# Two-layer transformer block: the weights of layer 0 prepared beside its first sequence, and a few steps of layer 1's rounds at other pairs

## The chip, the cores and the metric

The kernel is one program on one core of a Trainium2 chip. The time is that of one execution on the device, in microseconds; a kernel is timed in several runs, and their median stands for it. The profile is one more execution, recorded by the hardware.

Engines: PE (TensorE) does matrix products and transposes, PEld is its weight load, DVE is VectorE, ACT is ScalarE, POOL is GpSimd, SP issues transfers. PEclk is the clock that was granted to TensorE, as a share of 2.4 GHz; 0.50 is its lower level, 1.2 GHz.

## What is computed

x has 16 sequences of 512 tokens with 128 features. Two layers run one after the other, each with an attention-like part and a feed-forward part, both fed from the layer norm of x:

```
xn = layernorm(x);  x = x + L0_attn(xn) + L0_ffn(xn)
xn = layernorm(x);  x = x + L1_attn(xn) + L1_ffn(xn)

L0_attn: y = layernorm(xn) * ln1_g + ln1_b;  q, k, v = y @ W + b (128 -> 1024);  g = sigmoid(y @ Wg + bg)
         state = decay * state + k * v (a scan over tokens);  x2 = xn + (g * q * state * scale) @ Wo + bo
         out = x2 + gelu(layernorm(x2) @ W1 + b1) @ W2 + b2
L0_ffn:  h = silu(x w1 s1) * (x w2 s2);  gelu(h h1);  gelu(. h2);  . w3
L1_attn: gated linear attention in chunks of 64, 4 heads, RMS norm of o, gate, @ Wo
L1_ffn:  softmax attention with 16 heads of 8 over all 512 tokens, layer norm, router (one of 4 experts), layer norm
```

Products whose precision matters are made in three parts: each operand is split into a rounded part (_hi) and a rest (_lo), and hi x hi, hi x lo and lo x hi are summed.

## The kernel before

**Layer 0** is `layer0_program`. It has four blocks of engine programs, one after the other, with a barrier between them:

1. constants: SP loads the columns, rows, identity and plain weights, VectorE and ScalarE make small constants (L701 to L715);
2. `prepare_weights` (L41): the weights that are to be split come in five chunks into two raw buffers (SP, L61). For each chunk TensorE multiplies the blocks of 128 columns with a bias vector, 36 products in all, each in two passes of hardware (L70, x72 in the trace). Then ScalarE scales the chunk in place (L80), and VectorE casts it to the high part (L96) and subtracts that for the low part (L98);
3. the bias sums (L731 to L734);
4. `layer0_sequences` (L161): rounds r = -1 to 17. In a round each stage works on another sequence. Stage P (statistics, xn, transposes xT and yT, the gates of the ternary feed-forward) is one sequence ahead of stage M (v, k, g, q products, scan, output product). Round -1 has stage P of the first sequence alone. TensorE's first product of round 0 is `v` of the first sequence, reading yT_hi and w_hi (L353). Within round -1 VectorE has the statistics (L535), GpSimd a chain for 1/sqrt (L615 to L627), VectorE xn and yh (L546, L548), TensorE their transposes (L359), ScalarE the copy xT_hi (L463), VectorE xT_lo (L502), and then four gates with two products each, ScalarE L473 and L435, VectorE L562, L566, L502. Stage W, in rounds 0 to 2, splits weights for layer 1 ("prep" steps), with buffers prep_raw and prep.

**Layer 1** runs in rounds, 16 of which are full; a round has 32 pairs of steps, laid out by hand in `attention_order()`, a table of (pair, stage, step). A stage's step belongs to the sequence that is so many rounds behind. Every engine goes through the table in the same order. Pair p always begins with `score` p (L1325, two products, exponentiated by ScalarE into c_prob, L1444) and `max` p (L1307, two products, reduced by VectorE to c_row_max, L1597). Score p+1 needs exp p to be done, since there is one bank pair for it, and max p+1 needs reduce p. Then come `pv` (L1335), and what the table puts at the pair. The names that matter here:

- h2 n: half of a gate product of the feed-forward, six products (L1196 to L1198), at the pairs H2_AT;
- U, A: the chunk states (L1247, evaluated on VectorE L1559 to L1564) and the in-chunk scores (L1257, masked by VectorE into c_a_sb, L1569);
- xT: transposes of the next sequence (L1214);
- mT 0, m_st 0: transposes of the row maxima (L1313) and their store;
- aoT 3: transposes of the softmax attention's output (L1343); behind them VectorE has the reciprocal (L1603) and the division (L1605);
- oT, gwo: transposes of o (L1282), copied by ScalarE to c_o_f, and the output product (L1289), to which `r1` adds (L1591);
- rank, place: counting tokens per expert (L1296, L1662);
- gz: the first step of pair 0 (L1169).

Products other than score, max and pv take their PSUM bank from a ring of two, banks 6 and 7, in turn: a use waits until the use before it in the same bank was read. A round has 31 such uses.

Of the kernel before, what the change touches and what calls it, by code (L numbers as in the profile page):

```python
# [40 lines left out]
def prepare_weights(nc, name, raw_dram, split_hi, split_lo, chunks, bias_products=None, psum_bias=None, by_dim=(), base=0):  # L41

    widest = max(n for _, n, _ in chunks)
    with ExitStack() as ctx:
        raw = [ctx.enter_context(nc.sbuf_tensor(f"{name}_raw{i}", [P, widest * P], F32)) for i in range(2)]
        loaded = [ctx.enter_context(nc.semaphore(f"{name}_loaded{i}")) for i in range(2)]
        multiplied = ctx.enter_context(nc.semaphore(f"{name}_multiplied"))  # L50
        scaled = ctx.enter_context(nc.semaphore(f"{name}_scaled"))
        hi_done = ctx.enter_context(nc.semaphore(f"{name}_hi_done"))
        lo_done = ctx.enter_context(nc.semaphore(f"{name}_lo_done"))
        block = ctx.enter_context(nc.Block())

        @block.sync
        def _(sp):
            for i, (first, n, _) in enumerate(chunks):
                if i >= 2:
                    sp.wait_ge(lo_done, i - 1)  # L60
                sp.dma_start(raw[i % 2][:, 0:n * P], raw_dram[:, first * P:(first + n) * P]).then_inc(loaded[i % 2], 16)  # L61

        @block.tensor
        def _(pe):
            for i, (first, n, _) in enumerate(chunks):
                pe.wait_ge(loaded[i % 2], 16 * (i // 2 + 1))
                for blk, col, vec in bias_products or []:
                    if first <= blk < first + n:
                        w = raw[i % 2][:, (blk - first) * P:(blk - first + 1) * P]
                        nc.tensor.matmul(psum_bias[:, col:col + 1], w, vec, start=True, stop=True)  # L70
                pe.drain().then_inc(multiplied, 1)

        @block.scalar
        def _(act):
            for i, (first, n, scale) in enumerate(chunks):
                w = raw[i % 2][:, 0:n * P]
                act.wait_ge(loaded[i % 2], 16 * (i // 2 + 1))
                act.wait_ge(multiplied, i + 1)
                if scale is not None:
                    nc.scalar.activation(w, w, ACT.Copy, scale=scale).then_inc(scaled, 1)  # L80
                else:
                    act.drain().then_inc(scaled, 1)

        @block.vector
        def _(dve):
            for i, (first, n, _) in enumerate(chunks):
                w = raw[i % 2][:, 0:n * P]
                at = slice((first - base) * P, (first - base + n) * P)
                if first in by_dim:
                    w = w.rearrange("p (g j d) -> p g d j", j=4, d=8)  # L90
                    hi, lo = (s[:, at].rearrange("p (g d j) -> p g d j", d=8, j=4) for s in (split_hi, split_lo))
                else:
                    hi, lo = split_hi[:, at], split_lo[:, at]
                dve.wait_ge(loaded[i % 2], 16 * (i // 2 + 1))
                dve.wait_ge(scaled, i + 1)
                nc.vector.tensor_copy(hi, w).then_inc(hi_done, 1)  # L96
                dve.wait_ge(hi_done, i + 1)
                nc.vector.tensor_tensor(lo, w, hi.bitcast(F32), ALU.subtract).then_inc(lo_done, 1)  # L98
# [2116 lines left out]
```

## Time and profile before

| | us |
|---|---|
| median of 3 runs | 2697.13 |
| lowest and highest | 2694.82, 2701.45 |
| the profiled execution | 2709.48 |
| its span in the trace | 2707.7 |
| its mean granted clock | 0.956 |
| TensorE busy | 2422.3 (89%) |
| VectorE busy | 1933.5 (71%) |
| ScalarE busy | 1338.1 (49%) |

Layer 0's rounds begin at 74 us, full rounds of layer 1 (from one gwo to the next) at 1141.58 us; the last round ends with the output from GpSimd. In a timeline row the first number is the start, the second how long, and the bracket how long the engine had been idle before and what ended that. "x4" are instructions put together.

### The profile page before, as it was taken

What the parts mean: (1) busy time and instruction counts of PE and PEld (TensorE: products, weight loads), DVE (VectorE), ACT (ScalarE), POOL (GpSimd) and SP (SyncE); (2) the same over time, 40 slices, a digit from 0 to 9 for tenths busy, and PEclk for the clock granted to TensorE, in tenths of its full rate; (3) what the DMA queues carried; (4) which work ended last, traced back from release to release, by engine and by line L of the source; (5) the groups of instructions that cost most, each with busy time, mean ns of one, the idle gap of its engine ahead of it and who ended that gap; (6) DMA issues with size and microseconds to landing.
All of it is one profiled execution on the core that took longest, in us unless ns stands there. A gap on an engine that the chain in (4) does not pass through costs nothing. (4 is left out here: it accounts for less than half of the span.)

```text
span 2707.7 us, 45139 instructions
## 1 busy us (share of the span) xinstructions
PE 2422.3 (89%) x14582; PEld 1672.5 (62%) x14582; DVE 1933.5 (71%) x3706; ACT 1338.1 (49%) x1926; POOL 594.3 (22%) x630
## 2 busy tenths in 40 slices
PE   3899999999999946899999999999999999999596
PEld 2788888888888734654555545554555555554395
DVE  3889888888888713667777777777777777772375
ACT  1444444444444312265666656665666666555242
POOL 0021112111221100102222221213221221212287
PEclk9999999999999968999999999999999999999798
DMA  4334432233223133323343334333333233211463
GB/s 153 125 115 127 127 100 76 76 119 104 80 76 111 43 135 98 101 75 96 118 130 93 86 101 136 99 88 104 117 116 103 82 107 106 65 51 32 140 228 104
DMA packets 195550, 280.31 MB, mean 104 GB/s; under 512 B 21672, under 2 KB 151161, under 8 KB 186880
## 3 DMA queue, kind: packets, MB, share of 16 engines
q1 hardware_dynamic: 189952, 266.47, 32.8%
q0 software_dynamic: 5504, 12.63, 1.3%
q8 instruction: 53, 0.87, 0.1%
q14 instruction: 41, 0.34, 0.0%
HBM read 148.65 MB, written 131.91 MB: 104 GB/s over the span
## 5 line engine op out<-in xcount | busy, mean ns | idle before, releaser
L1597 DVE TENSOR_REDUCE c_row_max<-b_psum 128x2 f32<-128x1024 f32 x512 | 624.3, 1219 | 286.2 <-PE b_psum L1307 264.7
L1444 ACT ACTIVATE c_prob<-b_psum 128x1024 f32<-128x1024 f32 x512 | 524.1, 1024 | 388.0 <-PE b_psum L1325 384.4
L1307 PE MATMUL b_psum<-c_bk,c_bq 24*128 24x512 f32 x1024 | 261.8, 507 | 55.1 <-DVE c_row_max L1597 38.5
L1325 PE MATMUL b_psum<-c_cq,c_ck 25*128 25x512 f32 x1024 | 261.3, 505 | 36.4 <-ACT c_prob L1444 31.5
L1335 PE MATMUL b_psum<-c_prob,c_v_aug 128*32 128x512 f32 x2048 | 283.5, 627 | 0.3
L1325 PEld LDWEIGHTS b_psum<-c_cq,c_ck 25*128 25x128 f32 x1024 | 96.3, 185 | 218.1 <-ACT c_prob L1444 109.7
L353 PE MATMUL a_psum<-a_yT_hi,a_w_hi 128*128 128x512 f32 x512 | 206.8, 404 | 8.3 <-issue 5.9
L353 PE MATMUL a_psum<-a_yT_hi,a_w_lo 128*128 128x512 f32 x512 | 203.7, 398 | 0.0
L353 PE MATMUL a_psum<-a_yT_lo,a_w_hi 128*128 128x512 f32 x512 | 203.6, 398 | 0.0
L1307 PEld LDWEIGHTS b_psum<-c_bk,c_bq 24*128 24x128 f32 x1024 | 97.0, 186 | 108.1 <-DVE c_row_max L1597 82.1
L459 ACT ACTIVATE a_g<-a_psum,a_cols 128x512 f32<-128x512 f32 x64 | 44.1, 689 | 238.5 <-PE a_psum L353 238.5
L517 DVE TENSOR_TENSOR_SCAN a_st_sb<-a_decay,a_kv_sb 128x512 f32<-128x512 f32 x128 | 157.2, 1228 | 4.4
L615 POOL TENSOR_TENSOR a_rs<-a_mv,a_eps 128x4 f32<-128x4 f32 x16 | 3.2, 201 | 664.2 <-DVE a_mv L540 664.2
L376 PEld LDWEIGHTS a_psum<-a_w_plain,a_outs 128*128 128x128 f32 x1024 | 134.3, 192 | 11.8
L1196 PE MATMUL b_psum<-c_g_hi,b_f_hi 128*128 128x512 f32 x256 | 119.4, 467 | 17.7 <-DMA b_f_lo<-f_split_scratch 11.6
L376 PE MATMUL a_psum<-a_w_plain,a_outs 128*128 128x128 f32 x1024 | 135.0, 275 | 0.0
L1749 POOL TENSOR_TENSOR c_o_ms<-c_o_ms,b_minus_half 128x16 f32<-128x16 f32 x16 | 46.6, 2910 | 385.0 <-DVE c_o_ms L1581 385.0
L514 DVE SCALAR_TENSOR_TENSOR a_kv_sb<-a_psum,a_bias,a_v_sb 128x512 f32<-128x512 f32 x128 | 95.5, 746 | 44.0 <-PE a_psum L353 23.2
L353 PEld LDWEIGHTS a_psum<-a_yT_hi,a_w_hi 128*128 128x128 f32 x512 | 97.1, 190 | 29.8 <-issue 8.7
L447 ACT ACTIVATE a_v_sb<-a_psum,a_bias 128x512 f32<-128x512 f32 x128 | 88.7, 693 | 47.2 <-PE a_psum L353 46.2
L353 PEld LDWEIGHTS a_psum<-a_yT_lo,a_w_hi 128*128 128x128 f32 x512 | 97.6, 191 | 23.2
L353 PEld LDWEIGHTS a_psum<-a_yT_hi,a_w_lo 128*128 128x128 f32 x512 | 97.6, 191 | 21.2
(298 smaller groups left out, 5419.9 us busy)
## 6 DMA issues: line engine op xcount, KB each, us to landing
sorted_scratch<-a_pad SPq DMA_DIRECT2D x16, 2184.5 KB, 13.9
g_scratch<-a_g_hi SPq DMA_DIRECT2D x16, 1024.0 KB, 4.0
g_scratch<-a_g_lo SPq DMA_DIRECT2D x16, 1024.0 KB, 7.1
c_g_hi<-g_scratch SPq DMA_DIRECT2D x16, 1024.0 KB, 6.1
c_g_lo<-g_scratch SPq DMA_DIRECT2D x16, 1024.0 KB, 8.1
stack_scratch<-c_qk_hi SPq DMA_DIRECT2D x256, 64.0 KB, 1.6
d_wt<-expert_scratch SPq DMA_DIRECT2D x19, 834.0 KB
c_bq<-stack_scratch SPq DMA_DIRECT2D x128, 96.0 KB
```

Of the source, the lines that this page charges most:

```text
L353: mm = nc.tensor.matmul(out, a, c, start=(n == 0), stop=(n == last))
L376: mm = nc.tensor.matmul(tok[:, cut(t)], outs[:, i % OUTS, cut(t)], blk(w_plain, A_WO + i), start=(i == 0 and t == 0), stop=(i == FB0 - 1), ...
L447: nc.scalar.activation(v_sb[:, i % 2, :], bank(f"v{i}"), ACT.Identity, bias=bias[:, 4 * i:4 * i + 1]).then_inc(S["v"], 1)
L514: nc.vector.scalar_tensor_tensor(out=kv_sb[:, :], in0=bank(f"k{i}"), scalar=bias[:, 4 * i + 1:4 * i + 2], in1=v_sb[:, i % 2, :], op0=ALU.a ...
L517: nc.vector.tensor_tensor_scan(st_sb[:, :], decay[:, i:i + 1].to_broadcast([P, SEQ]), kv_sb[:, :], 0.0, ALU.mult, ALU.add).then_inc(S["sca ...
L1196: nc.tensor.matmul(bank(f"h2{c}"), hi, g1_hi[:, k, :], start=(k == 0), stop=False)
L1307: mm = nc.tensor.matmul(psum[:, MAX + x, :], bq[r, j, cut(t)], bk[r, j, :], start=True, stop=True)
L1325: mm = nc.tensor.matmul(psum[:, SCORE + x, :], ck[r, j, cut(kb)], cq[r, j, :], start=True, stop=True)
L1335: mm = nc.tensor.matmul(psum[32 * g:32 * g + 32, PV, :], v_aug[:, kb, HPG * j + g, :], prob[:, (2 * i + g // 2) % 4, g % 2, :], start=(kb ...
L1444: nc.scalar.activation(prob[:, i % 4, :, :], psum[:, SCORE:SCORE + 2, :], ACT.Exp, scale=DH1 ** -0.5).then_inc(S["exp"], 1)
L1597: nc.vector.tensor_reduce(row_max[:, t, at:at + 3:2], psum[:, MAX:MAX + 2, :], AX.X, ALU.max).then_inc(S["row_max"], 1)
L1749: nc.gpsimd.tensor_tensor(o_ms[:, 2, :], o_ms[:, 1, :], minus_half[:, :], ALU.pow).then_inc(S["o_rms"], 1)
```

## The change

In layer 0 the first three blocks are gone. Their work stands in `layer0_sequences`:

- SP issues, at its start, the loads of cols, the first sequence, the identity, then five raw chunks: s (128x1024), q1 and q2 (128x2048 each), h1 (into the space of a_ga), w1 (128x512), then the plain weights and rows;
- in round -1 ScalarE makes each high part by one Copy with scale from the raw weights (HIGH_BEHIND says behind which step), and VectorE each low part by one instruction raw x column - high (LOW_BEHIND);
- the 36 bias products stand between TensorE's steps of round -1 (BIAS_BEHIND), into bank 7;
- VectorE scales the output weights and adds the biases at the start of round 0; TensorE waits there for all five low parts, the biases and the scaling;
- the preparation for layer 1 uses the raw weights' space, and its first load waits until the last low part and bias product are done.

In layer 1's table h2 4 moves from pair 14 to 13. At the even pairs (2, 4, 6, 10, 16, 20) h2 stands first among the table's steps, at the odd ones last. mT 0 moves from pair 17 to 22, m_st 0 from 19 to 24, the second half of oT from 29 to 30. The ring is turned once in a round: O1 and the use behind it, mT 0, have the same bank, and so the uses before it have the other bank than they had, and gwo and the next round's gz share bank 6. The diff, cut:

```diff
+HIGH_BEHIND = {("stats", 0): ("s", "q1", "q2"), ("gate", 0): ("h1",), ("gate", 1): ("w1",)}
+LOW_BEHIND = {("stats", 0): ("s",), ("xn", 0): ("q1",), ("gate", 0): ("q2",), ("gate", 1): ("h1",), ("gate", 2): ("w1",)}
+BIAS_BEHIND = {("stats", 0): range(0, 8), ("xT", 0): range(8, 12), ("gate", 0): range(12, 18), ("gate", 1): range(18, 24),
+               ("gate", 2): range(24, 30), ("gate", 3): range(30, 36)}
...
+        raw = sb("raw", [P, A_H1 * P])
...
-        prep_raw = sb("prep_raw", [P, HID * P])
-        prep = sb("prep", [P, 2, HID * P], F32R)
+        prep_raw = raw[:, 0:HID * P]
+        prep = raw[:, HID * P:3 * HID * P].rearrange("p (h w) -> p h w", h=2).bitcast(F32R)
...
+            sp.dma_start(cols[:, :], d_cols).then_inc(S["cols_in"], 16)
+            sp.dma_start(xin[:, :, :], x_rows[0]).then_inc(S["x_in"], 16)
+            sp.dma_start(ident[:, :], d_ident).then_inc(S["ident_in"], 16)
+            for name in WEIGHTS:
+                sp.dma_start(raw_of[name], weight(d_split, name)).then_inc(S["raw_" + name], 16)
+            sp.dma_start(w_plain[:, :], d_plain[:, 0:A_W3 * P]).then_inc(S["plain_in"], 16)
+            sp.dma_start(rows[:, :, :], d_rows).then_inc(S["rows_in"], 16)
...
+                if not looped and add == 0:
+                    pe.wait_ge(S["w_lo"], len(WEIGHTS))
+                    pe.wait_ge(S["bias"], 3)
+                    pe.wait_ge(S["wo_scaled"], 1)
...
+                def weights_high(kind, i):
+                    for name in HIGH_BEHIND.get((kind, i), ()):
+                        act.wait_ge(S["raw_" + name], 16)
+                        by = WEIGHTS[name][2]
+                        nc.scalar.activation(weight(w_hi, name), raw_of[name], ACT.Copy,
+                                             scale=col(by) if by else 1.0).then_inc(S["w_hi"], 1)
...
+                def weights_low(kind, i):
+                    for name in LOW_BEHIND.get((kind, i), ()):
+                        dve.wait_ge(S["w_hi"], list(WEIGHTS).index(name) + 1)
+                        by = WEIGHTS[name][2]
+                        nc.vector.scalar_tensor_tensor(out=weight(w_lo, name), in0=raw_of[name], scalar=col(by) if by else 1.0,
+                                                       in1=weight(w_hi, name).bitcast(F32), op0=ALU.mult,
+                                                       op1=ALU.subtract).then_inc(S["w_lo"], 1)
...
-H2_AT = (2, 4, 6, 10, 14, 16, 19, 20)
+H2_AT = (2, 4, 6, 10, 13, 16, 19, 20)
...
+    for n, p in enumerate(H2_AT):
+        if p % 2 == 0:
+            put(p, "F", "h2", n)
     put(0, "C2", "xnb_ld")
...
-    put(17, "B", "mT", 0)
+    put(22, "B", "mT", 0)
...
-    put(19, "B", "m_st", 0)
+    put(24, "B", "m_st", 0)
...
-    put(29, "A1", "oT", 1)
+    put(30, "A1", "oT", 1)
...
+        ring_uses = [u for step in order for u in attention_uses(step)]
...
+        bank_of |= {u: RING[(n + 1) % 2] for n, u in enumerate(ring_uses[:ring_uses.index("O1") + 1])}
```

How the rows stand on the engines. In the fences, a row is the line, the operation, its output and inputs, the shape and the waits. Some semaphores of the hardware are used by several blocks, and then the name printed can be that of another block.

VectorE at the start of the program. Before, from the last chunk of weights to the first statistics:

```order
L96 CAST a_w_hi<-a_raw 128x2048 [waits a_scaled,a_loaded0]
L98 TENSOR_TENSOR a_w_lo<-a_raw,a_w_hi 128x2048 [waits a_hi_done]
L47 UNCONDITIONAL_BRANCH
L729 UNCONDITIONAL_BRANCH [waits barrier_Pool_Activation_PE_DVE_SP_release]
L731 TENSOR_TENSOR a_bias<-a_psum,a_cols 128x32
L732 TENSOR_TENSOR a_bias<-a_psum,a_cols 128x4
L734 TENSOR_SCALAR a_half_bias<-a_bias 128x32 [waits a_bias_done]
L725 UNCONDITIONAL_BRANCH
L487 UNCONDITIONAL_BRANCH [waits barrier_Pool_Activation_PE_DVE_SP_release]
L489 MEMSET a_pad 128x257
L491 MEMSET a_pad 128x1 [waits a_pad_set]
L535 BN_STATS a_stats<-a_xin 128x6 [waits a_x_in]
```

VectorE in the changed kernel, from the last yh of the first sequence:

```order
L583 TENSOR_SCALAR a_yh<-a_xin,a_mv,a_rs 128x128
L524 SCALAR_TENSOR_TENSOR a_w_lo<-a_raw,a_cols,a_w_hi 128x2048 [waits a_w_hi]
L518 TENSOR_TENSOR a_xT_lo<-a_psum,a_xT_hi 128x512 [waits a_xT_hi]
L597 SCALAR_TENSOR_TENSOR a_gate_w<-a_gate_t,a_psum 128x512 [waits a_gate_t]
L601 SCALAR_TENSOR_TENSOR a_h<-a_psum,a_s_half,a_gate_w 128x512 [waits a_gate_w,a_P_filled]
L524 SCALAR_TENSOR_TENSOR a_w_lo<-a_raw,a_cols,a_w_hi 128x2048 [waits a_w_hi]
```

The low parts of the weights, which all stood ahead of the statistics, now stand behind them, between the steps of the first sequence.

TensorE in pairs 13 and 14 of a round, from U on. Before:

```order
L1247 MATMUL b_psum<-c_v_sb,c_kgT 32x64 x12
L1321 REGISTER_ALU
L1325 MATMUL b_psum<-c_cq,c_ck 128x512 x2
L1303 REGISTER_ALU
L1307 MATMUL b_psum<-c_bk,c_bq 128x512 x2
L1164 ISA
L1257 MATMUL b_psum<-c_qg,c_kg 128x128 x8
L1164 REGISTER_ALU
L1196 MATMUL b_psum<-c_g_hi,b_f_hi 128x512
```

TensorE in the changed kernel, from U on:

```order
L1235 MATMUL b_psum<-c_v_sb,c_kgT 32x64 x12
L1152 REGISTER_ALU
L1184 MATMUL b_psum<-c_g_hi,b_f_hi 128x512
L1185 MATMUL b_psum<-c_g_hi,b_f_lo 128x512
L1186 MATMUL b_psum<-c_g_lo,b_f_hi 128x512
L1184 MATMUL b_psum<-c_g_hi,b_f_hi 128x512
L1185 MATMUL b_psum<-c_g_hi,b_f_lo 128x512
L1186 MATMUL b_psum<-c_g_lo,b_f_hi 128x512
L1309 REGISTER_ALU
L1313 MATMUL b_psum<-c_cq,c_ck 128x512 x2
```

The six products of h2 4, which stood behind A (L1257), now stand ahead of score 14; max 14, A, score 15 and max 15 follow without them.

TensorE at the end of a round, from the second half of oT or the rank to gwo. Before:

```order
L1282 MATMUL b_psum<-b_ident,c_o_n 128x128 [waits c_attn]
L1282 MATMUL b_psum<-b_ident,c_o_n 128x128 x3
L1321 REGISTER_ALU
L1325 MATMUL b_psum<-c_cq,c_ck 128x512 [waits c_exp]
L1325 MATMUL b_psum<-c_cq,c_ck 128x512
L1303 REGISTER_ALU
L1307 MATMUL b_psum<-c_bk,c_bq 128x512 [waits c_row_max]
L1307 MATMUL b_psum<-c_bk,c_bq 128x512
L1296 MATMUL b_psum<-c_ahead,c_ones_row 128x20 [waits c_o_f,c_ahead]
L1298 MATMUL b_psum<-c_mask,b_causal 128x16
```

```order
L1289 MATMUL b_psum<-b_w_plain,c_o_f 128x128 [waits c_o_f]
L1289 MATMUL b_psum<-b_w_plain,c_o_f 128x128 x7
L1031 REGISTER_ALU
L1031 COMPARE_AND_BRANCH
L1325 MATMUL b_psum<-c_cq,c_ck 128x512 [waits c_m_in0,c_exp,c_c_in0,c_ones_in]
L1325 MATMUL b_psum<-c_cq,c_ck 128x512
L1307 MATMUL b_psum<-c_bk,c_bq 128x512 [waits c_row_max,c_b_in0]
L1307 MATMUL b_psum<-c_bk,c_bq 128x512
L1169 MATMUL b_psum<-c_xT_hi,b_w_hi 128x512 [waits c_r1]
```

TensorE in the changed kernel at the same places:

```order
L1284 MATMUL b_psum<-c_ahead,c_ones_row 128x20 [waits c_attn,c_ahead]
L1286 MATMUL b_psum<-c_mask,b_causal 128x16
L1270 MATMUL b_psum<-b_ident,c_o_n 128x128 [waits c_o_f]
L1270 MATMUL b_psum<-b_ident,c_o_n 128x128 x3
L1309 REGISTER_ALU
```

```order
L1277 MATMUL b_psum<-b_w_plain,c_o_f 128x128 [waits c_place,c_o_f]
L1277 MATMUL b_psum<-b_w_plain,c_o_f 128x128 x7
L1019 REGISTER_ALU
L1019 COMPARE_AND_BRANCH
L1313 MATMUL b_psum<-c_cq,c_ck 128x512 [waits c_m_in0,c_exp,c_c_in0,c_ones_in]
L1313 MATMUL b_psum<-c_cq,c_ck 128x512
L1295 MATMUL b_psum<-c_bk,c_bq 128x512 [waits c_row_max,c_b_in0]
L1295 MATMUL b_psum<-c_bk,c_bq 128x512
L1157 MATMUL b_psum<-c_xT_hi,b_w_hi 128x512 [waits c_o_f]
```

The second half of oT now stands behind the rank; gwo waits for place besides the copy of o, and gz (the last row) for the copy of o instead of for r.

## Rows read from the trace of the kernel before

**Rows 1.** The page: TensorE busy, share, instructions; granted clock in 40 slices.

```profile
PE 2422.3 (89%) x14582; PEld 1672.5 (62%) x14582; DVE 1933.5 (71%) x3706; ACT 1338.1 (49%) x1926; POOL 594.3 (22%) x630
...
PEclk9999999999999968999999999999999999999798
```

**Rows 2.** Windows of the start: stretch, length, busy (instructions), clock, DMA share, GB/s.

```profile
13.20:46.50 33.30, 15.83 (x72) 15.58 (x72) 13.95 (x13) 4.72 (x3) 0.00 (x0) 1.00 0.21 78
46.50:74.20 27.70, 10.02 (x33) 6.24 (x33) 12.72 (x33) 7.34 (x11) 3.04 (x7) 1.00 0.73 210
```

**Rows 3.** Timeline of the first sequence in layer 0.

```profile
51.55 0.87 DVE L535 BATCH_NORM_STATS2 a_stats<-a_xin 128x6 f32<-128x128 f32 x4 [4.44 <-DMA a_xin<-in_x]
...
60.44 0.69 DVE L502 TENSOR_TENSOR a_xT_lo<-a_psum,a_xT_hi 128x512 fp32r<-128x512 f32 x1 [1.83 <-ACT a_xT_hi L463]
...
74.19 0.47 PE L353 MATMUL a_psum<-a_yT_hi,a_w_hi 128*128 128x512 f32 x1 [2.36 <-DVE a_yT_lo L502]
```

**Rows 4.** Transfers issued from 7 to 46.5: count, KB each, median us to landing.

```profile
a_raw<-in_a_split SPq DMA_DIRECT2D x3, 1024.0 KB, 6.8
```

**Rows 5.** Groups by line and shape, start: count, busy us, mean ns of one.

```profile
L98 DVE TENSOR_TENSOR a_w_lo<-a_raw,a_w_hi 128x2048 fp32r<-128x2048 f32 x3 | 6.9, 2293 | 0.1
...
L80 ACT ACTIVATE a_raw<-a_raw,a_cols 128x2048 f32<-128x2048 f32 x2 | 4.0, 2001 | 18.0 <-PEq L71 18.0
...
L566 DVE SCALAR_TENSOR_TENSOR a_h<-a_psum,a_s_half,a_gate_w 128x512 f32<-128x512 f32 x4 | 3.0, 751 | 0.5
```

**Rows 6.** Windows of two attention rounds, columns as in rows 2.

```profile
1578.81:1664.43 85.62, 79.08 (x545) 44.31 (x542) 65.15 (x119) 53.83 (x75) 21.04 (x20) 0.98 0.36 108
2277.29:2366.06 88.77, 83.34 (x545) 46.15 (x542) 65.00 (x119) 49.68 (x66) 21.06 (x20) 0.94 0.29 81
```

**Rows 7.** Windows of the ten low stretches in pairs 13 to 16, one and their sum.

```profile
1880.80:1887.60 6.80, 6.80 (x34) 3.60 (x32) 4.34 (x8) 1.02 (x1) 3.63 (x3) 0.50 0.04 13
...
sum 51.00, PE 50.97 PEld 28.40 DVE 34.91 ACT 7.20 POOL 29.37; mean PE 5.10 PEld 2.84 DVE 3.49 ACT 0.72 POOL 2.94
```

**Rows 8.** Windows from U to the first mq product, in two rounds.

```profile
1616.40:1630.00 13.60, 11.44 (x117) 6.51 (x110) 11.46 (x25) 5.78 (x8) 6.04 (x7) 1.00 0.26 74
1877.60:1894.30 16.70, 14.52 (x117) 7.99 (x109) 11.54 (x25) 5.76 (x8) 6.01 (x7) 0.80 0.29 79
```

**Rows 9.** Timeline of pairs 14 to 18 of one round.

```profile
1880.52 1.86 PE L1257 MATMUL b_psum<-c_qg,c_kg 32*128 32x128 f32 x16 [0.91 <-DVE c_states L1564]
...
1882.41 1.29 DVE L1569 TENSOR_TENSOR c_a_sb<-b_psum,b_causal 128x512 f32<-128x512 f32 x2 [0.81 <-PE b_psum L1257]
...
1883.62 1.11 DVE L1496 TENSOR_SCALAR c_xn<-c_x,c_mv,c_rs 128x128 f32<-128x128 f32 x4
...
1893.16 0.60 PE L1313 MATMUL b_psum<-b_ident,c_row_max 128*8 128x128 f32 x4
```

**Rows 10.** TensorE's waits from 1232 to 2367: waited for, total us, times, longest.

```profile
PE b_psum L1257 <- DVE c_states L1564: 11.6, 13, 0.9
PE b_psum L1214 <- DVE c_a_sb L1569: 8.3, 13, 0.6
```

**Rows 11.** Timeline: score 23 of a round.

```profile
1910.13 0.50 PE L1325 MATMUL b_psum<-c_cq,c_ck 25*128 25x512 f32 x2 [0.89 <-ACT c_prob L1444]
```

**Rows 12.** Timeline of pairs 4 to 6 of a round.

```profile
1853.96 1.22 DVE L1597 TENSOR_REDUCE c_row_max<-b_psum 128x2 f32<-128x1024 f32 x1 [1.83 <-PE b_psum L1307]
...
1855.11 0.24 DVE L1603 RECIPROCAL c_den<-b_psum 128x16 f32<-128x16 f32 x1
...
1859.68 0.50 PE L1307 MATMUL b_psum<-c_bk,c_bq 24*128 24x512 f32 x2 [0.34 <-DVE c_row_max L1597]
```

**Rows 13.** Timeline of a round's end and the next one's start.

```profile
1928.77 2.05 PE L1289 MATMUL b_psum<-b_w_plain,c_o_f 128*128 128x128 f32 x16
...
1929.23 0.16 DVE L1662 TENSOR_TENSOR b_place<-b_place,b_psum 128x4 f32<-128x4 f32 x1
...
1931.78 0.51 PE L1169 MATMUL b_psum<-c_xT_hi,b_w_hi 128*128 128x512 f32 x1 [0.52 <-DVE c_r L1591]
```

More of the change, by code:

```diff
@@ L38 @@
 OUT_SCALE0 = 0.5 * DH0 ** -0.5
[L41 to L98, printed above, removed]
@@ L232, in layer0_sequences @@
         sems("P_filled", "M_filled", "T_filled", "wo_done")
+        sems("cols_in", "ident_in", "rows_in", "plain_in", "consts", "decay", "w_hi", "w_lo", "bias_sum", "bias", "wo_scaled")
+        sems(*("raw_" + name for name in WEIGHTS))
         sems("gate_t", "h0_hi", "v", "t", "g1", "hT_hi", "ga", "xT_hi", "yT_hi")
@@ L346, in take, with bias_products @@
                             return
+                def bias_products(kind, i):
+                    steps = [step[1:] for step in now]
+                    at = steps.index((kind, i))
+                    for n in BIAS_BEHIND.get(steps[at - 1], ()) if at else ():
+                        if n in (0, 16, 32):
+                            pe.wait_ge(S["raw_" + ("q1", "q2", "w1")[n // 16]], 16)
+                        block, by = (A_QKVG + n, "ln1_b") if n < 4 * FB0 else (A_W1 + n - 4 * FB0, "ln2_b")
+                        mm = nc.tensor.matmul(tok[:, n:n + 1], blk(raw, block), col(by), start=True, stop=True)
+                        if n == 4 * FB0 + HID - 1:
+                            mm.then_inc(S["bias_sum"], 1)
                 def product(out, w_blocks, x_hi, x_lo):
@@ L360, in turned @@
                     return mm
+                if not looped and add == 0:
+                    pe.wait_ge(S["w_lo"], len(WEIGHTS))
+                    pe.wait_ge(S["bias"], 3)
+                    pe.wait_ge(S["wo_scaled"], 1)
                 for stage, kind, i in now:
                     filled = S.get(stage + "_filled")
+                    if not looped and add == -1:
+                        bias_products(kind, i)
                     if kind in ("v", "k", "g", "q"):
@@ L397, in rounds @@
                     elif kind == "gate":
+                        if i == 0 and not looped and add == -1:
+                            pe.wait_ge(S["w_lo"], 1)
                         if i == 0:
@@ L597, in rounds @@
                                                 ALU.add).then_inc(S["x1"], 1)
+                    if isinstance(base, int) and add == -1:
+                        weights_low(kind, i)
             run(dve, rounds)
@@ L736, in layer0_program @@
-        layer0_sequences(nc, psum, w_hi, w_lo, w_plain, col, bias, half_bias, decay, rows, ident, s1_half, s12_half, minus_half, eps,
-                         d_x, d_x1, d_g1, d_sorted, prep_chunks, table_parts)
+        layer0_sequences(nc, psum, w_hi, w_lo, w_plain, cols, bias, half_bias, decay, rows, ident, s1_half, s12_half, minus_half, eps,
+                         d_x, d_split, d_plain, d_cols, d_rows, d_ident, d_x1, d_g1, d_sorted, prep_chunks, table_parts)
 GH, GDK, GDV = 4, 32, 64
@@ L844, in attention_order @@
     for n, p in enumerate(H2_AT):
-        put(p, "F", "h2", n)
+        if p % 2:
+            put(p, "F", "h2", n)
     for t, p in enumerate(W3_AT):
```

99 lines of the change are left out of this document (49 added, 50 removed).

## Prediction

> **What bounds the kernel now.** I read the engine busy times first, then the stretches up to the first steady work, then the attention rounds one by one. TensorE is busy 2422.3 of 2707.7 us, 89%, and its clock row shows a nine in nearly every slice: the kernel is long because TensorE has much to do, and time can be had only where it idles or runs slow [rows 1]. The stretches at the start show the first kind. Until 13.2 TensorE waits for the first weights; in the 33.3 us that follow it is busy 15.83 us with the one-column bias products, and in the 27.7 us after that 10.02 us [rows 2]. The first projection that the rounds are made of starts at 74.19 [rows 3]. So 74 us are a prologue in which no engine is full: VectorE has 13.95 us of work in the middle 33.3.
>
> The attention rounds show the second kind. A round takes 85.6 us where the granted clock averages 0.98 and 88.8 where it averages 0.94, with the same 545 matmuls and the same 65 us of VectorE [rows 6]. The difference sits in one place: in pairs 13 to 16 of most rounds the clock stands at 0.50, the 1.2 GHz level, for 3.4 or 6.8 us at a time; ten such stretches make 51.0 us of the thirteen rounds from 1230.91 to 2366.06, and TensorE is busy through all of them (50.97) [rows 7]. The same 117 matmuls of those pairs take 13.60 us at 1.00 and 16.70 at 0.80 [rows 8], so a low stretch of 6.8 us costs 3.1, and 51.0 us cost 23. Right before the stretch at 1880.80 TensorE had waited 0.91 us for the states [rows 9].
>
> **The prologue.** Before, it is serial: constants, then weights (bias products, scaling, cast, subtraction, chunk by chunk), then the bias sums, and only then the load of the first sequence, for which VectorE waits 4.44 us, until 51.55 [rows 3]. The change puts this load second in SP's queue, so that the first statistics start after the same wait and half a microsecond for what stands ahead, about at 5. From landing to the first projection the kernel before takes 74.19 - 51.55 = 22.6 us. If the weights cost nothing, the first projection would stand at 5 + 22.6 = 27.6, a gain of 46.6. What they still cost:
> - Transfers. Up to the second 1 MB chunk SP issues 0.35 + 0.5 + 1 + 1 = 2.85 MB. Two 1 MB loads in flight land after 6.8 us [rows 4], that is 3.4 us per MB; 9.7 us plus some 2 for issue and first bytes puts that chunk at about 12.5. At the 210 GB/s of the stretch from 46.5 it would be 16 [rows 2].
> - ScalarE makes the high parts with one pass each (2.00 us for 2048 columns [rows 5]), and the pass of the second chunk stands ahead of the copy of the transposed input. The pass ends at 14.5 to 16 and the copy, a quarter as wide, half a microsecond later, at 15.0 to 16.5. VectorE's subtraction behind the copy would begin at 5 + (60.44 - 51.55) = 13.9 [rows 3]: a delay of 1.1 to 2.6 us.
> - VectorE makes the low parts with one scaled subtraction. No row shows it 2048 wide: a plain subtraction of that width is 2.29 us, and a row with three inputs is 0.751 at 512 wide, four of which are 3.0 [rows 5]. I take 2.3: at 512 wide the two kinds are near (0.751 against 0.69 [rows 3]), and the plain one needs 2.29 for four times the width, less than 4 x 0.69, so part of a short one is fixed. The small chunk fits into VectorE's wait for GpSimd's chain; the first large one into the wait for the transposes. Behind that stand 2.3 + 2.3 + 0.7, the output weights' scaling of 0.7 and the bias sums of 0.5: 6.5 us (7.9 at the high price). The gates' own VectorE work there is 8 passes of 0.69 to 0.75 and 5 subtractions of 0.69 [rows 3, 5], 9.2 us of the 13.1 from the end of the subtraction behind the copy (60.44 + 0.69) to 74.19, so up to 3.9 us of it is covered. Cost 2.6 to 7.9.
> - The 36 bias products lie between the first TensorE steps, 36 x 0.22 = 7.9 us (72 of them were 15.83), in the 17.7 us that TensorE idles there [rows 2]; nothing. If that cover went, 3 to 4 us of them would show.
> Sum: first projection at 27.6 + (3.7 to 10.5) = 31.3 to 38.1, at the slow transfer rate, 2 to 3 us more, 41. I take 36, the upper middle, because the new first projection waits for all low parts and VectorE is in order. **Gain 38, bounds 33 to 43.** Nothing behind it shrinks: the order of layer 0's rounds is the same. The preparation loads now wait in SP's queue for the last low part, since they use the raw weights' space; behind them on SP stand only the stores of their own chunk and of layer 0's outputs, and the first chunk is read by a step of round 0 that comes after its first projections. TensorE's new waits ahead of round 0 (low parts, bias, output weights) are in the 36; queued behind them is all of round 0.
>
> **The rounds of layer 1, at the high clock.** Per round, from a round's rows:
> - Pairs 13 to 18. The gate product of pair 14 now stands between U and score 14, and one before xT. That covers the waits for the states (11.6 us in 13 rounds, 0.89 each) and for a_sb (8.3, 0.64) [rows 10]; mT 0, four transposes of 0.60 us [rows 9], leaves too; I count 0.53 of it, since the next score starts beside its end. But score and max 15 come straight behind, and before max 16 TensorE then has pv, A and a score, an estimated 2.6 us, while VectorE has a_sb 1.29, xn 1.11 and the reduce 1.22 [rows 9, 12]: a new wait of 1.1. Net -2.06 + 1.1 = -0.9.
> - mT 0 at pair 22 goes into the 0.89 us that TensorE waits for exp 22 [rows 11]: nothing; without that cover 0.53 comes back.
> - Pairs 4 to 9. The gate product of pair 4 now stands ahead of aoT 3. Its six products last an estimated 1.6 us; the reciprocal behind that transpose began as reduce 4 ended (1853.96 + 1.22, 1855.11) and moves by 0.9 with all that VectorE has queued behind it (attn, the log-sigmoid, the scans, reduce 5). Max 6 waited 0.34 for that reduce already [rows 12], so TensorE loses 0.9, and 0.2 more at exps 7 and 8. Cost +1.1.
> - Round's end. Behind the turn of the ring gz waits for the copy of o, long done, and no longer for r (0.52 [rows 13]). In exchange gwo waits for the addition to place, which began 0.46 us after gwo did [rows 13]: with its 0.16 and the way back +0.65. The two halves of oT now stand a pair apart, which takes about 0.45 from the wait for exp 30. Net -0.3.
> Together -0.1 per round; each term can be off by half a microsecond, so 14 rounds give **-1, bounds -8 and +6**.
>
> **The low stretches.** What goes before a fall is the wait between U and A. It is now filled with six products. I expect the falls in pairs 13 to 16 to go in most rounds: **-19** of the 23, bounds 0 and -23. The new wait of 1.1 us stands where the falls were, which is what speaks against it. The trace shows the fall right behind a wait of 0.91 [rows 9], within pairs that idle for 1.5 us in all [rows 10]. The Trainium skill ("TensorE: Matmul & The Clock Gate", section "A second HAM failure mode: psum-queue depth-cycling") describes a kernel in which frequent short idles between groups of matmuls made the clock swing between its two levels, and the loss was in the throughput, not in a single matmul. By that rule it is the number of short idles that counts; here two go and one of 1.1 us comes, the swing would stay, and the sum would be 2658 rather than 2640.
>
> **Sum.** The profiled execution took 2709.5 us, 12.4 above the median of the three runs, 2697.1. 2709.5 - 38 - 19 - 1 = 2651.5; less 12.4 it is 2639, say 2640.
>
> **Rivals.**
> - The prologue's gain alone (0.28). The 1.1 us wait at max 16 takes the role of the two that went, and the clock falls there as before. For: the falls are in ten places of thirteen rounds, and the order is the same in the rounds that stay at 0.98, so that TensorE stands close to the edge. Against: the idle time of those pairs goes from 1.5 us to 1.1. 2697 - 38 - 1 = 2658. The rule of the page named above speaks for this case.
> - The stalls go and no new one comes (0.08), because VectorE takes xn later than I have it or pair 4 finds slack. Then 0.89 + 0.64 + 0.53 = 2.1 us for 13 rounds, 27, in place of 1: 2697 - 38 - 19 - 27 = 2613.
> - Half the prologue (0.07). The ten loads share the queues with each other, and the low parts wait for them; the first projection comes at 50 to 60 rather than 36, and the lull goes or stays: 2697 - (14 to 24) - (0 to 19) = 2654 to 2683.
> - Slower (0.05). The delay of VectorE's chain in pairs 4 to 9 opens a wait of 1.2 us at max 6 in every round, the clock falls there for 6.8 us (3.1 lost) as it does now in pairs 13 to 16, and those falls stay. (3.1 + 1.1) x 14 = 59: 2697 - 38 + 59 = 2718. Against the gain of 38 it decides from (38 - 15) / 3.1, eight of the 14 rounds. Against: max 6 waits 0.34 now [rows 12], and the ten stretches of rows 7 lie all in pairs 13 to 16.
>
> **Chances.** Forecast 0.52. The range goes from 2620 (the bounds of the forecast's terms, -43 and -8, part of them) to 2668 (the second case with the prologue at its bound of 33 and some of the +6) and leaves out 0.2. Differences under 0.3%, 8 us, can't be told from none. Faster by more than that: the first four cases, 0.93, after something for their tails; within 0.3% 0.03; slower 0.04.
>
> **What would show it.** The first projection between 31 and 41, and bias products between the first gates. No stretch at 0.50 in pairs 13 to 16 and 11 or more of 13 rounds near 85.5 us; A no longer waiting for the states, max 16 waiting 1.1 us for the maxima, max 6 some 1.2. The waits of gz for r gone, one of gwo for place there. Wrong it would be if the rounds kept their three lengths (the clock), if rounds at 0.98 were over 86.2 or under 85 (the walk), or if the first projection came after 42 (transfers or VectorE).

## The result, and the profile after

| | before | after |
|---|---|---|
| median, us | 2698.28 (4 runs) | 2662.10 (4 runs) |
| lowest and highest | 2694.82, 2701.45 | 2660.20, 2668.52 |
| ratio, with 95% interval | | 0.987 [0.985, 0.989] |
| span of the profiled execution | 2707.7 | 2658.4 |
| mean granted clock in it | 0.956 | 0.958 |
| first projection of layer 0 | 74.19 | 33.67 |
| thirteen rounds of layer 1 | 1135.15 | 1132.76 |

The change takes 36 us off, where 57 were forecast; the range of 2620 to 2668 holds the time. The two profiled executions are 49 us apart, more than the medians, because the one of before lay 11 us above its median.

The page of the changed kernel, engines and granted clock, answers to [rows 1]. TensorE is busy 91% of a shorter span, and its clock is no better:

```profile
PE 2409.5 (91%) x14582; PEld 1669.9 (63%) x14582; DVE 1925.5 (72%) x3701; ACT 1341.0 (50%) x1927; POOL 585.4 (22%) x630
...
PEclk9999999999999878999999999999999999999798
```

Windows and timeline of its start, for [rows 2] and [rows 3]: stretch, length, busy us of PE, PEld, DVE, ACT, POOL, clock, DMA share, GB/s.

```profile
0.00:13.20 13.20, 3.21 (x16) 3.24 (x17) 6.74 (x26) 5.44 (x5) 3.71 (x11) 1.00 0.81 290
13.20:33.67 20.47, 16.25 (x90) 13.98 (x91) 16.40 (x22) 9.47 (x13) 0.00 (x0) 0.97 1.08 301
```

```profile
4.28 0.87 DVE L570 BATCH_NORM_STATS2 a_stats<-a_xin 128x6 f32<-128x128 f32 x4 [1.38 <-DMA a_xin<-in_x]
...
11.91 2.35 DVE L524 SCALAR_TENSOR_TENSOR a_w_lo<-a_raw,a_cols,a_w_hi 128x2048 fp32r<-128x2048 f32 x1
...
12.31 2.00 ACT L429 ACTIVATE a_w_hi<-a_raw,a_cols 128x2048 fp32r<-128x2048 f32 x1 [0.43 <-DMA a_raw<-in_a_split]
...
15.14 0.69 DVE L518 TENSOR_TENSOR a_xT_lo<-a_psum,a_xT_hi 128x512 fp32r<-128x512 f32 x1 [0.88 <-ACT a_xT_hi L465]
...
33.67 0.76 PE L335 MATMUL a_psum<-a_yT_hi,a_w_hi 128*128 128x512 f32 x1 [3.03 <-DVE a_half_bias L537]
```

The statistics start at 4.28, the second 1 MB chunk is there at 12.31, xT_lo starts at 15.14 and the first projection at 33.67, behind VectorE's bias sums. VectorE is busy 16.40 of the last 20.47 us, and the 2048 wide row that no row of before showed costs 2.35 us.

Windows of two rounds of layer 1, for [rows 6], the shortest and the longest of the thirteen:

```profile
1184.10:1268.74 84.64, 77.79 (x546) 44.35 (x542) 64.98 (x118) 53.94 (x74) 16.89 (x15) 1.00 0.36 104
1617.06:1706.98 89.92, 83.28 (x541) 47.80 (x542) 65.08 (x119) 53.91 (x74) 21.02 (x20) 0.92 0.35 102
```

TensorE's waits in those rounds (what waited, for what, total us, times, longest), for [rows 10]:

```profile
PE b_psum L1295 <- DVE c_row_max L1585: 45.0, 63, 1.3
PE b_psum L1313 <- ACT c_prob L1432: 18.8, 69, 1.1
PE b_psum L1277 <- DVE b_place L1650: 8.3, 12, 0.7
PE b_psum L1245 <- DVE c_states L1552: 5.0, 13, 0.8
```

The wait of A for the states went from 0.89 to 0.4 us a round, the ones for a_sb and for r are gone but for one, and gwo waits 0.69 for place. The waits of the max products for VectorE's reduces have grown from 26.3 us to 45.0, those of the scores for the exps have shrunk from 25.5 to 18.8.

Timeline of pair 6 in one round, for [rows 12], and max 16 of another:

```profile
1812.99 0.50 PE L1295 MATMUL b_psum<-c_bk,c_bq 24*128 24x512 f32 x2 [1.26 <-DVE c_row_max L1585]
1813.42 0.50 PE L1184 MATMUL b_psum<-c_g_hi,b_f_hi 128*128 128x512 f32 x1
1813.76 0.39 PE L1185 MATMUL b_psum<-c_g_hi,b_f_lo 128*128 128x512 f32 x1
1813.99 0.44 PE L1186 MATMUL b_psum<-c_g_lo,b_f_hi 128*128 128x512 f32 x1
1814.22 0.63 PE L1184 MATMUL b_psum<-c_g_hi,b_f_hi 128*128 128x512 f32 x1
1814.65 0.63 PE L1185 MATMUL b_psum<-c_g_hi,b_f_lo 128*128 128x512 f32 x1
...
1926.07 0.50 PE L1295 MATMUL b_psum<-c_bk,c_bq 24*128 24x512 f32 x2 [0.90 <-DVE c_row_max L1585]
```

Here one sees what became of the low stretches. Max 6 waits 1.26 us, TensorE starts again with products of 0.39 us, and a microsecond later they take 0.63: the clock has fallen. Such a stretch lasts 3.4 us (once 6.8) and now comes 20 us into a round (pair 6), 46 us (pair 16) or 76 us (pair 27), and never at 40, where [rows 7] had them.

### The profile page after: what moved, and what is told of

The parts are those of the page before. It is cut to its first block and busy times, and to the rows that moved or that the text cites. A ratio compares the mean times of both kernels' runs of the same rounds, so it can differ in the third digit from the quotient of the medians.

```text
span 2658.4 us, 45097 instructions
## 1 busy us (share of the span) xinstructions
PE 2409.5 (91%) x14582; PEld 1669.9 (63%) x14582; DVE 1925.5 (72%) x3701; ACT 1341.0 (50%) x1927; POOL 585.4 (22%) x630
## 5 line engine op out<-in xcount | busy, mean ns | idle before, releaser
L364 PEld LDWEIGHTS a_psum<-a_w_plain,a_outs 128*128 128x128 f32 x1024 | 133.7, 191 | 11.7
L1184 PE MATMUL b_psum<-c_g_hi,b_f_hi 128*128 128x512 f32 x256 | 120.2, 470 | 19.1 <-DMA b_f_lo<-f_split_scratch 11.7
L562 DVE SCALAR_TENSOR_TENSOR a_outs<-a_t_sb,a_u_sb 128x512 f32<-128x512 f32 x128 | 103.8, 811 | 16.9
```

The source lines that it names most:

```text
L364: mm = nc.tensor.matmul(tok[:, cut(t)], outs[:, i % OUTS, cut(t)], blk(w_plain, A_WO + i), start=(i == 0 and t == 0), stop=(i == FB0 - 1), ...
L562: nc.vector.scalar_tensor_tensor(out=outs[:, i % OUTS, :], in0=t_sb[:, i % 2, :], scalar=1.0, in1=u_sb[:, :], op0=ALU.add, op1=ALU.mult).t ...
L1184: nc.tensor.matmul(bank(f"h2{c}"), hi, g1_hi[:, k, :], start=(k == 0), stop=False)
```

## How the rounds of the traces are read

Each kernel below has a trace, and twelve rounds of each (from the second gwo on, the rounds with all stages) were compared. For every round I took its length, the time at the low clock (read from windows of 0.85 us), and whether reduce 2, the third of a round, came late (a row of VectorE released by "remote", see the last section). The expectations call it the reduce of pair 3; pairs are counted from 0, and it is that of pair 2. Least squares over all 168 rounds, with one full-clock length for each order of the rounds, gives: length = full-clock length + 0.35 x us at the low clock + 1.17 if reduce 2 is late; the lengths are left with a scatter of 0.36 us, the full-clock lengths are good to 0.1. "Low" is us at the low clock per round. The columns "at ..." count rounds, of twelve, with a fall in that stretch of the round, to a microsecond; falls elsewhere, most of them 5 us into a round, are in "low" alone.

| kernel | full-clock round | low | at 20-23 | at 39-44 | at 45-51 | at 74-80 | late | median us | ratio to before |
|---|---|---|---|---|---|---|---|---|---|
| before | 84.77 | 5.0 (with e1) | 0 | 10 | 0 | 1 | 5 | | 1 |
| e1, prologue alone | same | | 0 | 8 | 0 | 3 | 5 | 2661.4 | 0.9855 [0.982, 0.989] |
| after | 84.76 | 5.7 (with e2) | 9 | 0 | 8 | 6 | 0 | 2662.1 | 0.987 [0.985, 0.989] |
| e2, rounds alone | same | | 6 | 0 | 7 | 2 | 8 | 2702.9 | 1.002 [1.000, 1.004] |
| e3, pair 4 | 83.50 | 4.0 | 0 | 0 | 3 | 8 | 8 | 2654.1 | 0.985 [0.982, 0.988] |
| e4, rank behind oT | 84.00 | 5.4 | 5 | 0 | 5 | 5 | 6 | 2656.5 | 0.984 [0.981, 0.987] |
| e5, h2 at 15 | 84.86 | 3.1 | 3 | 0 | 1 | 2 | 6 | 2667.7 | 0.987 [0.985, 0.989] |
| e6, all three | 82.88 | 2.8 | 0 | 0 | 0 | 6 | 5 | 2635.3 | 0.974 [0.973, 0.976] |
| e7, scatters first | 83.22 | 2.8 | 0 | 0 | 0 | 5 | 0 | 2635.7 | 0.974 [0.972, 0.976] |
| e8, score 6 three times | 84.82 | 3.7 | 4 | 0 | 6 | 2 | 7 | 2666.4 | 0.985 [0.984, 0.987] |
| e9, score 6 six times | 84.55 | 1.7 | 0 | 0 | 2 | 4 | 7 | 2662.3 | 0.990 [0.986, 0.993] |
| e10, reduce 5 twice | 84.08 | 4.3 | 8 | 0 | 1 | 3 | 6 | 2657.8 | 0.986 [0.983, 0.989] |
| e11, mT 0 at 26 | 83.01 | 1.4 | 0 | 0 | 1 | 0 | 6 | 2630.2 | 0.976 [0.973, 0.979] |
| e12, e11 and e7 | 83.59 | 0.6 | 0 | 0 | 1 | 0 | 0 | 2633.9 | 0.977 [0.975, 0.979] |

The runs came in several groups on different chips, where the kernel before took between 2694.2 and 2705.7 us, so that the ratios compare better than the medians. A trace is one execution, and traces of one order differ: before and e1 have 5.4 and 4.6 us at the low clock in a round, after and e2 6.8 and 4.6, and "late" is 0 in after and 8 in e2. e1 to e4 ran together (before: 2696.6), e5 to e8 (2705.7), e9 to e11 (2694.2), and e12 alone (2696.4).

## The experiments

The theory after the result: the prologue brought what was forecast, the new order costs and gives nothing at full clock, and the low stretches follow TensorE's longer waits for VectorE, so that removing two of these and making two new ones only moved them. The rival: the clock falls so and so often under this load, whatever the waits.

**e1_prologue**: the changed kernel with attention_order() and the ring of before.

> The joined preparation of layer 0 alone; layer 1's rounds as before. If the parts add, this takes 38 to 41 us off the kernel before (first projection at 33.7, as in the changed kernel) and the thirteen rounds keep their sum of about 1135 us with the low-clock stretches in pairs 13 to 16: near 2658. Rival: the measured 36 us hide a larger prologue gain eaten by slower rounds or the reverse; then this is clearly under 2655 or over 2666.

2661.4 us, ratio 0.9855: 39 us less than before (30 to 48). The first projection starts at 35.63.

**e2_rounds**: the kernel before with the new attention_order() and the new ring.

> The new order and ring of layer 1 alone; layer 0 as before. If the rounds are a wash (0.5 us more each at full clock, as many low-clock stretches as before at other pairs, no late reduce in pair 3), the ratio to before is 0.998 to 1.004. Rival: the order gains as the trace pair says (49 us less in the traces against 36 in the medians), then 0.995 to 0.997. Low stretches are expected at 20, 46 and 77 us into a round, none at 40.

Ratio 1.002, just above 1 in its interval. The parts add: 0.9855 + 0.002 = 0.9875 against 0.987. The low stretches stand where the changed kernel has them, with the old prologue in front.

**e3_pair4**: the gate product of pair 4 behind aoT 3 again.

```diff
     for n, p in enumerate(H2_AT):
-        if p % 2 == 0:
+        if p % 2 == 0 and p != 4:
             put(p, "F", "h2", n)
```

> The changed kernel with the gate product of pair 4 behind aoT 3 again. Cover theory: the wait of max 6 goes from 1.26 to 0.35 us, a round loses 0.9 us at full clock, and the low-clock stretch at 20 us into the round goes from most rounds (8 of 13 had it, 1.3 to 1.5 us each): 14 x 0.9 + 10 = some 22 us under the changed kernel, near 2640. Rival, the clock falls a fixed number of times whatever the waits: the stretch turns up elsewhere, and only 12 us are gained, near 2650. Third: nothing is gained, since the late reduces of pair 3 come back (1.5 us in half of the rounds).

A full-clock round is 1.26 us shorter and no fall is left at 20-23, as the cover theory has it. But at 74-80 there are eight, and reduce 2 is late in eight rounds, where the changed kernel's trace had none (e2, with the changed kernel's order, has eight too); of the 22 us it expected the ratio shows 6 (0.9847 against 0.987, intervals that overlap), the thirteen rounds of the traces 16.

**e4_rank**: the rank behind the second half of oT, so that gwo finds its bank free.

```diff
-    put(30, "C2", "rank")
...
     put(30, "A1", "oT", 1)
+    put(30, "C2", "rank")
```

> The changed kernel with the second half of oT ahead of the rank in pair 30, so that gwo shares its bank with oT and not with the rank. The wait of gwo for place (0.69 us, 13 of 13 rounds) goes, 14 x 0.65 = 9 us: near 2653. Rival: score 31 then waits longer for exp 30, behind which ScalarE has the copy of o (0.3 to 0.6 us a round), and 0 to 4 us are left of it.

gwo's wait is gone from the trace, and a full-clock round is 0.76 us shorter. The ratio moves by 0.0027, 7 us of the 9 expected, but within the intervals.

**e5_h2_15**: the gate product of pair 16 at pair 15.

```diff
-H2_AT = (2, 4, 6, 10, 13, 16, 19, 20)
+H2_AT = (2, 4, 6, 10, 13, 15, 19, 20)
```

> The changed kernel with the gate product of pair 16 at pair 15. Cover theory: it fills TensorE's wait of 0.90 us at max 16, xT then waits 0 to 0.2 for the mask, a round at full clock goes from 84.66 to about 83.9 us, and no low-clock stretch starts at 46 us into a round: 9 us under the changed kernel, some 5 more from the clock. Rival, xT and the scores behind it wait for VectorE's mask in its place (0.6): 0 to 3 us.

TensorE's waits over its thirteen rounds:

```profile
PE b_psum L1295 <- DVE c_row_max L1585: 36.0, 53, 1.3
PE b_psum L1313 <- ACT c_prob L1432: 25.5, 79, 1.1
```

9 us went from the waits for maxima and 6.7 came back at the exps: the full-clock round stays (84.86), which is the rival. The falls at 45-51 go from 15 in 24 rounds (after, e2) to one in 12, though a wait of 0.6 us for an exp has taken the place of the 0.90.

**e6_three**: e3, e4 and e5 together.

> The changed kernel with all three: pair 4's gate product behind aoT 3, the rank behind oT, pair 16's product at pair 15. If the three add, a full-clock round is 84.66 - 1.22 - 0.75 - 0.75 = 81.9 to 82.0 us, 38 us less over 14 rounds, and the low-clock stretches are left at 75 us alone: 2620 to 2625. Rival, VectorE becomes the bound and the waits come back elsewhere: a round over 83, 2640.

Full-clock round 82.88; the three differences, -1.26, -0.76 and +0.10, sum to 82.84. Ratio 0.974, 34 us less than the changed kernel: 14 x 1.88 = 26 from the order, and 14 x 0.35 x (5.7 - 2.8) = 14 from the clock, together somewhat more than was timed. Only the falls at 74-80 and four at 5 us are left. It beats both kernels.

**e7_scatter**: GpSimd's scatters ahead of its addition.

```diff
-    put(31, "A1", "r1b")
     put(31, "C2", "scatter")
+    put(31, "A1", "r1b")
```

> The kernel of the run before with GpSimd's four scatters ahead of its addition at pair 31. If the late reduce of pair 3 (1.1 us, in 28 of 72 rounds) comes from a scatter that GpSimd issues while the reduce is due, the scatters are over 2 us sooner and no late reduce is left: 3 to 8 us under it. Rival, it depends on something else: late reduces in as many rounds, same time.

No reduce is late by the table's sign, but the full-clock round is 0.34 us longer, and 1.17 x 5/12 = 0.49 a round is about what that gives back: the same time. Part of the delay is still there under another name: reduce 2 starts 7.8 to 8.0 us into a round in six of the twelve rounds of e7 and in ten of e12, and at 7.1 to 7.3 in all twelve of the changed kernel.

**e8_fill** and **e9_full**: score 6 issued two, or five, more times before the one that counts. They go into the same bank ahead of it, so that TensorE does products nobody needs in the place where it waited.

```diff
+                            for _ in range(5 * (i == 6)):
+                                nc.tensor.matmul(psum[:, SCORE + x, :], ck[r, j, cut(kb)], cq[r, j, :], start=True, stop=True)
```

> The changed kernel with score 6 of each round computed three times instead of once: 0.86 us of idle TensorE at max 6 becomes work that nobody needs. If the clock falls because TensorE idles there, the stretch at 20 us (9 of 13 rounds) is gone or rare and the kernel is 5 to 12 us faster although it does more; full-clock rounds stay at 84.7. Rival, the fall has to do with the place or the sort of work: the stretch stays and the time is the changed kernel's or up to 5 us more.

> The changed kernel with score 6 computed six times instead of once: 2.15 us of products where TensorE waited 1.24 for max 6. A round at full clock gets some 0.9 us longer (85.6). Idle theory: TensorE doesn't idle there at all, so no low-clock stretch starts at 20 to 22 us (where the order stood like this and the wait was 1.2, 23 of 48 rounds had one), which gives back 8 of the 13 us: about 5 us over the changed kernel. Rival, the order of the work brings the fall and not the idling: stretches in about half of the rounds, 13 us over.

e8 is inconclusive: the wait at max 6 shrank from 1.24 only to 0.78 us, and 4 of 12 rounds have the fall, not clearly fewer than the 23 of 48 of after, e2, e4 and e5. In e9 the wait is gone. TensorE's timeline of pair 6:

```profile
1814.29 1.54 PE L1314 MATMUL b_psum<-c_cq,c_ck 25*128 25x512 f32 x8
1815.55 0.38 PE L1315 MATMUL b_psum<-c_cq,c_ck 25*128 25x512 f32 x1
1815.67 0.61 PE L1314 MATMUL b_psum<-c_cq,c_ck 25*128 25x512 f32 x2
1816.05 0.50 PE L1295 MATMUL b_psum<-c_bk,c_bq 24*128 24x512 f32 x2
```

Max 6 starts 1.76 us after the first score product, as in the changed kernel (1811.23 to 1812.99 there), with work in place of the idling, and no round of twelve has a fall at 20-23. So a round did not get the 0.9 us longer that I had expected. The low clock falls to 1.7 us a round, and the trace is as long as the changed kernel's (2657.8) although it does 160 more products; the timed ratio, 0.990 [0.986, 0.993], is not below the changed kernel's, and the 8 us that the expectation wanted back can't be seen in it.

**e10_twice**: e6, and VectorE does reduce 5 twice, the first time into a tile that nobody reads.

```diff
+                        if i == 5:
+                            nc.vector.tensor_reduce(twice[:, :], psum[:, MAX:MAX + 2, :], AX.X, ALU.max)
```

> The kernel with the three edits, and VectorE does reduce 5 of each round twice (1.22 us more), so that max 6 waits 1.5 us instead of 0.35 with the same order of products. A round gets 0.9 to 1.2 us longer at full clock. Idle theory: low-clock stretches come back at 20 to 22 us in a third to a half of the rounds (none in 60 rounds where this wait was 0.35), 8 us: together some 22 us over it. Rival, the wait doesn't matter to the clock: 13 to 17 us over, no stretch there.

The order of TensorE's work is that of e6; only its wait at max 6 is longer. e6 and e10, the same place:

```profile
1795.99 0.50 PE L1295 MATMUL b_psum<-c_bk,c_bq 24*128 24x512 f32 x2 [0.35 <-DVE c_row_max L1585]
```

```profile
1819.22 0.51 PE L1296 MATMUL b_psum<-c_bk,c_bq 24*128 24x512 f32 x2 [1.51 <-DVE c_row_max L1588]
...
1820.45 0.40 PE L1185 MATMUL b_psum<-c_g_hi,b_f_hi 128*128 128x512 f32 x1
1820.69 0.56 PE L1186 MATMUL b_psum<-c_g_hi,b_f_lo 128*128 128x512 f32 x1
1821.05 0.63 PE L1187 MATMUL b_psum<-c_g_lo,b_f_hi 128*128 128x512 f32 x1
```

The falls are back, in 8 of 12 rounds; without it there is none in 12, and none in the 60 rounds of the five traces in which max 6 waits 0.35 us (e3, e6, e7, e11, e12). A full-clock round is 1.2 us longer, and the ratio is 0.986 against 0.974: 32 us, to some 8 either way, where 22 were expected; the thirteen rounds of the traces are 26 apart.

**e11_mT26**: e6 with mT 0 at pair 26, in front of the wait of max 27.

```diff
-    put(22, "B", "mT", 0)
+    put(26, "B", "mT", 0)
...
-    put(24, "B", "m_st", 0)
+    put(28, "B", "m_st", 0)
```

> The kernel with the three edits, and mT 0 at pair 26 instead of 22 (its store at 28). It fills the wait of max 27 (0.68 to about 0.15) and leaves the one of score 23 (0.35 to 0.9), so a round at full clock stays at 82.9. If the low-clock stretches at 75 us come from the wait at max 27, they go (6 of 12 rounds, 1.2 us each) and 5 to 8 us are gained: near 2629 on the scale of 2635. Rival, they come from the wait of score 23 then, at 67 us (0 of 24 rounds in the kernel before, with 0.89 us there), or the store comes too late for the next round: same time or slower.

The falls at 74-80 are gone (6 of 12 before, none now), two stand at 67 us instead. Thirteen rounds take 1095.95 us against 1097.89 of e6. The ratio, 0.976 [0.973, 0.979], can't be told from e6's.

**e12_all**: e11 and e7.

> The kernel with the three edits, mT 0 at pair 26 and the scatters ahead of the addition. If the effects seen one at a time add: a full-clock round 82.9 + 0.15 + 0.35 = 83.4, no late reduce, 1.4 us at the low clock in a round in place of 2.8, which is 0.5 us a round or 7 us less than with the three edits: a ratio to before of 0.971 to 0.973. Rival: the terms are at the edge of what can be told apart, ratio 0.974 to 0.976.

Two falls in twelve rounds and no late reduce; thirteen rounds take 1092.19 us, the shortest of all. Yet the ratio is 0.977 [0.975, 0.979], just beyond the rival's, and not below e6's 0.974 [0.973, 0.976]. In the two traces the rounds gain 5.7 us and the part up to the second gwo loses 7.7 (1192.56 against 1184.89), although both first projections start late, at 40.99 and 40.38; what makes that part longer is not known. e6 is the kernel I would keep.

## Why the prediction held in the prologue and failed in the rounds

**Prologue: right.** Forecast 38 (33 to 43); the trace shows 40.5, e1 alone 39 by its ratio. The chain went as walked: the chunk at 12.3 (forecast 12.5), xT_lo at 15.14 (15.0 to 16.5), the wide low parts 2.35 us each (2.3), the bias products under other work. The forecast for the chunk has a slip that happened to help: its terms, 9.7 and 2, add to 11.7 and not to 12.5. One thing was left out: TensorE's own pace. In six of the twelve traces with the new prologue the first projection starts at 33.7 to 35.9, in the other six at 40.4 to 41.2, the upper end of the bounds and a gain of 33 to 34 only. Windows from 24 to 28 us, e4 and then the changed kernel:

```profile
24.00:28.00 4.00, 4.00 (x17) 3.69 (x16) 3.88 (x4) 1.00 (x2) 0.00 (x0) 1.00 1.11 260
```

```profile
24.00:28.00 4.00, 2.80 (x19) 2.21 (x17) 3.88 (x5) 1.02 (x2) 0.00 (x0) 1.00 1.11 244
```

In e4 TensorE is busy all the time, and its products of 512 columns follow each other every 0.43 us as they do in the low stretches, though the clock column says 1.00; in the changed kernel they follow every 0.23. The 1.00 is no measurement: the trace has no record of the clock before 18.8 us in the changed kernel and before 44.3 in e4, and the column counts a stretch without a record as 1.00. The pace of the products changes where the records begin. The changed kernel on both sides of 18.8:

```profile
18.25 0.63 PE L335 MATMUL a_psum<-a_xT_lo,a_w_hi 128*128 128x512 f32 x1
...
20.31 0.39 PE L335 MATMUL a_psum<-a_xT_hi,a_w_lo 128*128 128x512 f32 x1
```

So TensorE starts every one of these traces at the lower pace. The records begin at 18.8 to 25.1 us in the six traces with the early projection and at 43.7 to 46.1 in the six with the late one; why they differ isn't shown. In the late ones the idling under which I had put the bias products is hardly there. e4, from 13.2 to its first projection:

```profile
13.20:41.02 27.82, 24.79 (x92) 22.07 (x93) 17.11 (x22) 9.95 (x13) 0.00 (x0) 1.00 0.90 249
```

TensorE is busy 24.79 of the 27.82 us and VectorE 17.11, so TensorE bounds the start there.

**Rounds at full clock: right, by parts.** Forecast -0.1 us a round, fitted 84.77 and 84.76. Max 6 waits 1.26 (forecast 1.2), max 16 0.90 (1.1), gwo 0.69 (0.65), gz no longer. e3 gives 1.26 for the delay at pair 4 (forecast 1.1), e4 0.76 for gwo's wait (0.65).

**The low stretches: wrong.** This is the term of -19 us, and the step that failed is to count the falls that go from pairs 13 to 16 as time gained, with nothing for falls at the new waits. They did go (18 of 24 rounds before and in e1, none in 144 after), but I let the clock depend on the waits that the change removes and not on those that it makes, although the same text forecast both new waits to 0.2 us. The falls moved to them: 15 of 24 rounds at pair 6 and 15 of 24 at pair 16 (after and e2). The time at the low clock went from 5.0 us a round to 5.7, that is +0.35 x 0.7 x 14 = 3 us instead of -19; as two traces of one order differ by 0.8 and 2.2 us a round, this says no more than that nothing was gained. The price was off too: by the fit the 51.0 us of [rows 7] cost 18 and not 23. Nor did the difference between the two rounds of [rows 6] sit in pairs 13 to 16: the long one has its low stretch 71 us into the round and a late reduce besides. Of the signs that were named, the one for the clock came (rounds of 84.6 to 89.9 us, where 11 of 13 were to be near 85.5), and the one for the walk did not in three of the four rounds at 0.98 (85.9 to 86.0, within 85 to 86.2; the fourth, the last of the thirteen, takes 87.3).

The Trainium skill ("TensorE: Matmul & The Clock Gate", "A second HAM failure mode: psum-queue depth-cycling") describes a clock that swings between its two levels when TensorE idles briefly and often between groups of products. The traces agree in that short waits in a busy TensorE are enough, and the time is near the 2658 that I had set for it. That the number of idles counts, as I had read it, they don't show: from e6 to e10 one wait of a round grows from 0.35 to 1.51 us, and the falls come. The rival "the prologue's gain alone" named max 16 as the new place and 2658 as the time, and had 0.28. The rival on the slower side named max 6, rightly; it needed eight more rounds with 6.8 us than before, and got stretches of 3.4 us in nine rounds while those of pair 14 went.

Added up: 2698.3 - 39 + 3 = 2662, against 2662.1. That it fits so closely is luck, since e1 gives its 39 only to 9 us either way. That the range holds the time is not: its upper end was set for the rival "the prologue's gain alone".

**What is shown and what isn't.** That idling at a place brings the fall there is shown from both sides: with the order kept, more waiting brings it (e6 to e10, 0 to 8 of 12), and with the order kept, work in place of the wait takes it away (23 of 48 rounds in after, e2, e4 and e5, 0 of 12 in e9). How long a wait must be is open. 0.68 us at max 27 was followed by a fall in some rounds, 0.89 us at score 23 in the kernel before [rows 11] in none of 24, though the same wait in e11 in 2 of 12.

## What to carry to other kernels

Where TensorE is nearly full, a change of order has to be judged by all waits that it leaves, not by the one it removes: each wait costs its own length and, now and then, 3.4 us at half clock behind it, 1.2 us by the fit. Put the products of a step that waits for nobody straight in front of the wait that VectorE's longest run of work makes, and check that they don't delay what VectorE needs next; here moving one such step back by four transposes (e3) gave 1.26 us a full-clock round, of which the timed runs alone could not be sure. A serial prologue is the surer gain: its sum could be read from rows and came out within 5 us in every trace.
